# A convolution and attention network on one core: the order of the calls in a step of the attention stage, arranged anew

## The reference

```python
queries = conv1x1_bn(x, wq, sq, bq).reshape(b, NUM_HEADS, KEY_DIM, hw)   # 8 heads of 32
kv = conv1x1_bn(x, wkv, skv, bkv).reshape(b, KEY_DIM, hw)
key = jax.nn.softmax(kv, axis=2)
query = jax.nn.softmax(queries, axis=2)
context = jnp.einsum('bkn,bdn->bkd', key, kv)
attended = jnp.einsum('bkd,bhkn->bhdn', context, query).reshape(b, MQ, h, w)
x = x + conv1x1_bn(jax.nn.relu(attended), wp, sp, bp)
hdn = conv1x1_bn(x, w1, s1, b1)                        # 96 -> 384 channels
hdn = jax.nn.relu(depthwise_3x3(hdn, wdw) + bdw)
x = x + conv1x1_bn(hdn, w2, s2, b2)                    # 384 -> 96
```

## Time and profile before

| | |
|---|---|
| Time, median of 3 runs | 6700.78 us |
| The profiled execution: its own time | 6705.41 us |
| The profiled execution: span, mean granted TensorE clock | 6703.6 us, 0.981 |
| Busy share of the span: PE, DVE, POOL, ACT | 90%, 82%, 71%, 57% |
| Attention stage, from the start to the first instruction of the next stage | 0 to about 1828 us |

### The profile page before, as it was taken

The page is one execution under the profiler, slowest core; times in us unless marked ns, Lnnn a source line. Parts: engine busy times, 40 slices in busy tenths (PEclk is TensorE's granted clock), DMA queues, the critical chain, the costliest instruction groups (busy, mean ns, idle before and its releaser), DMA issues. The chain is left out here.

```text
span 6703.6 us, 228614 instructions
## 1 busy us (share of the span) xinstructions
PE 6053.1 (90%) x96819; PEld 3479.4 (52%) x96819; DVE 5507.3 (82%) x8016; ACT 3811.1 (57%) x5690; POOL 4761.0 (71%) x3268
## 2 busy tenths in 40 slices
PE   7999999999779999999999999999999999996877
PEld 3444444444345555555555555655555665553333
DVE  5776776776578888888888888888888888886998
ACT  3444444444346666656666655666665666664776
POOL 2344333334258888888888888888888888886766
PEclk9999999999889999999999999999999999998999
DMA  1111111111100000010000010000001000001221
GB/s 30 43 46 41 53 43 46 46 42 47 34 26 3 3 3 3 3 44 3 3 3 3 3 35 13 3 3 3 3 3 44 3 3 3 3 3 50 71 75 52
DMA packets 115654, 157.60 MB, mean 24 GB/s; under 512 B 30512, under 2 KB 79952, under 8 KB 114768
## 3 DMA queue, kind: packets, MB, share of 16 engines
q1 hardware_dynamic: 114768, 144.38, 7.6%
HBM read 53.67 MB, written 52.79 MB: 16 GB/s over the span
## 5 line engine op out<-in xcount | busy, mean ns | idle before, releaser
L241 ACT ACTIVATE nn_yy<-nn_P 128x612 f32<-128x612 f32 x1200 | 817.0, 681 | 1656.8 <-DVE nn_P L330 1639.3
L397 PE MATMUL nn_P<-nn_hh,nn_w 64*64 64x256 f16 x38400 | 1534.8, 273 | 220.6 <-DVE nn_nl L341 107.1
L209 POOL TENSOR_TENSOR nn_hf<-nn_hf,nn_sr 128x512 f32<-128x512 f32 (+1 forms) x800 | 1439.9, 1821 | 155.4 <-DVE nn_sr L363 155.4
L220 POOL TENSOR_TENSOR nn_hl<-nn_hf,nn_hh 128x512 f16<-128x512 f32 (+1 forms) x768 | 1266.2, 1649 | 314.5 <-ACT nn_hh L253 306.3
L397 PEld LDWEIGHTS nn_P<-nn_hh,nn_w 64*64 64x64 f16 x38400 | 1022.7, 106 | 834.0 <-issue 664.7
L404 PE MATMUL nn_P<-nn_nh,nn_w 64*64 64x512 f16 x19200 | 1320.6, 379 | 77.6 <-DVE nn_nl L341 8.8
L330 DVE SCALAR_TENSOR_TENSOR nn_P<-nn_P,nn_xs 128x612 f32<-128x612 f32 x1200 | 960.4, 800 | 234.2 <-PE nn_P L397 209.6
L336 DVE TENSOR_TENSOR nn_P<-nn_P,nn_nh 128x612 f32<-128x612 f32 x1200 | 960.2, 800 | 213.2 <-ACT nn_nh L246 206.8
L397 PE MATMUL nn_P<-nn_hl,nn_w 64*64 64x256 f16 x19200 | 994.0, 270 | 1.5 <-issue 1.2
L341 DVE SCALAR_TENSOR_TENSOR nn_nl<-nn_P,nn_nh 128x612 f16<-128x612 f32 x1200 | 952.1, 793 | 34.3
L246 ACT ACTIVATE nn_nh<-nn_yy 128x612 f16<-128x612 f32 x1200 | 856.1, 713 | 37.9
(11 more groups left out here) (215 smaller groups left out, 7986.1 us busy)
## 6 DMA issues: line engine op xcount, KB each, us to landing
xn_scratch<-at_xb SPq DMA_DIRECT2D x128, 114.8 KB
nn_xs<-xn_scratch SPq DMA_DIRECT2D x48, 306.0 KB, 3.0
at_x<-in_x SPq DMA_DIRECT2D x32, 384.0 KB, 3.8
x_scratch<-at_x SPq DMA_DIRECT2D x64, 192.0 KB, 2.1
h_scratch<-nn_hf SPq DMA_DIRECT2D x48, 256.0 KB, 3.1
ml_xt<-x_scratch SPq DMA_DIRECT2D x32, 384.0 KB, 4.4
ml_ht<-h_scratch SPq DMA_DIRECT2D x128, 96.0 KB
out<-ml_ot SPq DMA_DIRECT2D x64, 192.0 KB, 2.1
```

The source lines that it names most:

```text
L209: e.tensor_tensor(hf[c][:, g, :], hf[c][:, g, :], sr[c][:, :].unsqueeze(1).broadcast_to((128, g.stop - g.start, A_COLS)), ALU.mult).then_i ...
L220: e.tensor_tensor(hl[c][:, g, :], hf[c][:, g, :], hh[c][:, g, :], ALU.subtract).then_inc(h_lo[n], 1)
L241: e.activation(half(yy[k % RING][:, :]), Pv[k % 2], ACT.Ln).then_inc(logged, 1)
L397: return pe.matmul(out[:, 0:AC, rows_y] if near else out[:, 1:BC, rows_y], w1[rows, wp, a, 1 if near else 0, k, cols], (hh, hl)[dp][u][row ...
```

## The change

In `attention_block` the five `step` lists are rewritten but for SP's: POOL, ACT, DVE and PE call the same functions for the same images, in another order, and part of them one step later than before. No function, wait, tile or transfer is changed. What comes a step later: on PE the blocks from `conv(i1, 1, 2)` on, which become `conv(i2, 1, 2)` to `conv(i2, 5, 2)`, `mix` of the blocks 1 to 3 and `e_sum` of block 3 (now of `i1`), both `mlp_out`, and of the normalisation both `x_sum` and the second half's `centring` and `variance` (now of `i3`). PE's list before and after:

```diff
-                project(i1, 0); conv(i2, 4, 2); centring(i2, 0); conv(i2, 5, 0); project(i1, 1); variance(i2, 0); conv(i2, 5, 1)
-                keys(i0); conv(i2, 5, 2); q_rows(i0, 0); conv(i1, 0, 0); q_rows(i0, 1); conv(i1, 0, 1); mlp_out(i2, 1)
-                k_turn(i0); conv(i1, 0, 2); x_sum(i2, 0); q_cols(i0, 0); conv(i1, 1, 0); context(i0); q_cols(i0, 1)
...
+                mix(i1, 1); conv(i2, 1, 2); conv(i2, 2, 0); e_sum(i1, 3); conv(i2, 2, 1); mix(i1, 2); conv(i2, 2, 2); conv(i2, 3, 0)
+                mix(i1, 3); x_sum(i3, 0); project(i1, 0); keys(i0); centring(i3, 1); project(i1, 1); variance(i3, 1); conv(i2, 3, 1)
+                conv(i2, 3, 2); conv(i2, 4, 0); q_rows(i0, 0); conv(i2, 4, 1); mlp_out(i2, 0); q_rows(i0, 1); conv(i2, 4, 2); x_sum(i3, 1)
+                k_turn(i0); q_cols(i0, 0); conv(i2, 5, 0); q_cols(i0, 1); context(i0); centring(i2, 0); q_cols(i0, 2); conv(i2, 5, 1)
+                e_sum(i0, 0); variance(i2, 0); conv(i2, 5, 2); q_cols(i0, 3); e_sum(i0, 1); conv(i1, 0, 0); mix(i0, 0); conv(i1, 0, 1)
+                conv(i1, 0, 2); conv(i1, 1, 0); conv(i1, 1, 1); mlp_out(i2, 1); e_sum(i0, 2)
```

The other three lists of the change, of which the prediction speaks too (POOL, ACT, DVE):

```diff
+                a_low(i2, 1); a_low(i2, 2); a_low(i2, 3); x1_low(i2, 0); hidden_low(i3, 2); x1_low(i2, 1); e_low(i1, 0); hidden_low(i3, 3)
+                e_low(i1, 1); hidden_low(i3, 4); e_low(i1, 2); hidden_low(i3, 5); x_low(i0); e_low(i1, 3); hidden_low(i2, 0)
+                hidden_low(i2, 1); a_low(i1, 0)

+                x_high(i0); log_e(i1, 2); inv_e(i1, 2); a_high(i1, 0); relu(i2, 1); log_e(i1, 3); inv_e(i1, 3); a_high(i1, 1); relu(i2, 2)
+                log_x(i3, 0); a_high(i1, 2); a_high(i1, 3); inv_x(i3, 0); square(i3, 1); x1_high(i1, 0); log_var(i3, 1); inv_root(i3, 1)
+                k_exp(i0); spread(i0, 0); x1_high(i1, 1); spread(i0, 1); relu(i2, 3); log_x(i3, 1); q_exp(i0, 0); relu(i2, 4)
+                q_exp(i0, 1); e_high(i0, 0); square(i2, 0); e_high(i0, 1); log_e(i0, 0); inv_e(i0, 0); log_var(i2, 0); inv_root(i2, 0)
+                relu(i2, 5); log_e(i0, 1); inv_x(i3, 1); q_exp(i0, 2); q_exp(i0, 3); inv_e(i0, 1); e_high(i0, 2); e_high(i0, 3)
+                relu(i1, 0)

+                refine_e(i1, 2); attended(i1, 2); back_e(i1, 3); x2_make(i3, 1); floor(i3, 0); refine_e(i1, 3); attended(i1, 3)
+                hidden_high(i2, 2); sum_clamp(i3, 0); x1_make(i1, 0); k_max(i0); k_negate(i0); back_x(i3, 0); k_copy(i0); refine_x(i3, 0)
+                var_a(i3, 1); x1_make(i1, 1); var_b(i3, 1); refine_root(i3, 1); scale(i3, 1); q_max(i0, 0); k_inv(i0); affine(i3, 1)
+                floor(i3, 1); q_max(i0, 1); divide(i3, 0); sum_clamp(i3, 1); k_place(i0); hidden_high(i2, 3); x2_make(i2, 0)
+                hidden_high(i2, 4); context_scale(i0); block_diag(i0); back_e(i0, 0); refine_e(i0, 0); hidden_high(i2, 5); var_a(i2, 0)
+                var_b(i2, 0); back_e(i0, 1); refine_root(i2, 0); back_x(i3, 1); attended(i0, 0); hidden_high(i1, 0); scale(i2, 0)
+                refine_x(i3, 1); affine(i2, 0); refine_e(i0, 1); back_e(i0, 2); hidden_high(i1, 1); attended(i0, 1); divide(i3, 1)
```

More of the change, by code:

```diff
@@ L786, in step @@
             def step(n, p, t):
[L787 to L790, removed]
+                i0, i1, i2, i3, = image(n, p, t, 0), image(n, p, t, 1), image(n, p, t, 2), image(n, p, t, 3)
+                a_low(i2, 1); a_low(i2, 2); a_low(i2, 3); x1_low(i2, 0); hidden_low(i3, 2); x1_low(i2, 1); e_low(i1, 0); hidden_low(i3, 3)
+                e_low(i1, 1); hidden_low(i3, 4); e_low(i1, 2); hidden_low(i3, 5); x_low(i0); e_low(i1, 3); hidden_low(i2, 0)
+                hidden_low(i2, 1); a_low(i1, 0)
             images(e, step)
@@ L1243, in step @@
             def step(n, p, t):
-                i0, i1, i2 = (image(n, p, t, 0), image(n, p, t, 1), image(n, p, t, 2),)
-                project(i1, 0); conv(i2, 4, 2); centring(i2, 0); conv(i2, 5, 0); project(i1, 1); variance(i2, 0); conv(i2, 5, 1)
-                keys(i0); conv(i2, 5, 2); q_rows(i0, 0); conv(i1, 0, 0); q_rows(i0, 1); conv(i1, 0, 1); mlp_out(i2, 1)
-                k_turn(i0); conv(i1, 0, 2); x_sum(i2, 0); q_cols(i0, 0); conv(i1, 1, 0); context(i0); q_cols(i0, 1)
[L1248 to L1251, removed]
+                i0, i1, i2, i3, = image(n, p, t, 0), image(n, p, t, 1), image(n, p, t, 2), image(n, p, t, 3)
+                mix(i1, 1); conv(i2, 1, 2); conv(i2, 2, 0); e_sum(i1, 3); conv(i2, 2, 1); mix(i1, 2); conv(i2, 2, 2); conv(i2, 3, 0)
[4 more added lines that the diff above has]
+                conv(i1, 0, 2); conv(i1, 1, 0); conv(i1, 1, 1); mlp_out(i2, 1); e_sum(i0, 2)
             images(e, step)
```

## The result

The change takes 6770.22 us (median of 4 runs, 6757.91 to 6780.92), the kernel before 6701.39 beside it (4 runs, 6697.58 to 6705.15): 1.0102 times as long, 95% interval 1.0083 to 1.0121, or 69 us more. The forecast was 6750. The profiled execution of the change is its slowest, 6780.92 us; that of before took 6705.41.

The account below looks back on a forecast made before the run. PE was taken to bound the attention stage. Removed waits -81 us, `block_diag` +87, `x_sum` +39 and ends +6 gave +51, some 48 with roundings; from a median of 6700.8 this made 6750 us, range 6650 to 6772.

Parts of the forecast that it names:

- What bounds the kernel: Attention stage: PE bounds it; a step of 54.06 us would take 51.3 us without PE's three waits.
- What the order removes: PE's waits for `pack`'s DMAs, `a_low` and `sum_clamp` in each step all go: -2.8 us a step.
- Rival D: SP's queue: late x2 puts `pack` behind `conv(i1, 0, 0)`, each further us costing 29 us; above 6772 us, chance 0.08.
- `block_diag`, +2.9 a step: DVE's last four pieces wait out POOL's gapless run, so PE waits 2.9 us at `e_sum(i0, 0)`; ends 0 and 3.3.
- Rival A: At `block_diag` the subtractions get in and cost nothing, `x_sum` still waits: 6665 us (6650 to 6685), chance 0.24.
- `x_sum`, +1.3 a step: At the step's end POOL delays `divide` on DVE, so `x_sum(i3, 0)` starts 1.3 us late; ends 0 and 2.
- The ends: Pipeline's start and end: -6 and -3 at the start, +13 and +1.5 at the end, about +6 us.
- The sum: Whole kernel: -81, +87 for `block_diag`, +39 for `x_sum`, +6 at the ends, together +51 us, some 48 with roundings.

Follow-up runs that it names:

- experiment 7: The kernel of experiment 1 with POOL's `a_low(i1, 0)` moved ahead of `hidden_low(i2, 1)`: 6647.97 us, ratio to the kernel before 0.9918.
- experiment 8: The kernel of experiment 7 with `floor(i3, 0)` also ahead of `x2_make(i3, 1)` on DVE: 6647.93 us, ratio to the kernel before 0.9915.
- experiment 1: The change with `block_diag`'s eight pieces reading the context from PSUM, applying the reciprocal themselves: 6669.91 us, ratio to the kernel before 0.9951.
- experiment 12: The change itself run once more, nothing altered: 6764.18 us, last stage 583.9 us.

## Why the prediction was right, and where its parts were off

The forecast (slower, 6750) had the right sign and mechanism and was 20 us low. That it came so near is in part luck: the errors of its terms in the steady steps cancel, as the last point shows. The median of 6770.22 lies 2 us inside the upper end of the range given, 6772.

- **What bounds the kernel; 51.3 us a step without waits.** Right: 51.33 in experiments 7 and 8, with PE idle for 0.2 us in all.
- **What the order removes, -2.8 a step.** Right (54.06 - 51.33 = 2.73): none of the three waits is left in the steps, and `pack` is in time. Rival D (the DMAs) didn't come.
- **`block_diag`, +2.9 a step.** The place holds, and the size nearly: the wait is 2.33 us, and a step at clock 1.00 is 54.67, 2.55 above that of experiment 1. What the prediction gave as its value's reason failed: "If the subtractions don't get in, they end at 7.8", with the casts running by and the subtractions shut out. The casts are hit as well, and every piece gets in behind one POOL instruction; that was the other end of this term, 3.3. The two readings give nearly one sum, since in both the last pieces come behind POOL's fourth instruction. Rival A (the subtractions get in, 6665) was wrong in taking it that getting in after one instruction is cheap for eight pieces. Its 6665 is what the kernel does once the collision is taken away (experiment 1, 6670).
- **Why `back_x` misled.** Among the rows of single DVE instructions, those that waited out most of one POOL instruction and then let POOL do a further one first are `back_x` before the change (13 in all, where the prediction counted 14; two further ones), and after it `refine_x` (28, one further) and one `affine` (line 998, one further). All 42 had come in the middle of an `x_low` (97 x 1024). One of them, timeline after the change:

```profile
1167.59 2.12 POOL L758 TENSOR_TENSOR at_x<-at_x,at_x 97x1024 f16<-97x1024 f32 x1 [0.68 <-ACT at_x L803]
1167.71 3.66 DVE L1022 SCALAR_TENSOR_TENSOR at_nr<-at_nt,at_ny 96x512 f32<-96x512 f32 x1
1169.67 1.16 POOL L770 TENSOR_TENSOR at_e<-at_e,at_e 128x512 f16<-128x512 f32 x1
```

  `refine_x` arrives behind the start of `x_low`, `e_low` goes first too, and it ends at 1171.37. It is a scalar_tensor_tensor, so the operation isn't the distinction; and `back_x` itself, where it meets an `e_low` after the change, gets in behind it, 25 times of 25. Behind a POOL instruction of any other line DVE was let in after one, where it had come more than 0.2 us before its end. (The other `refine_x` of a step comes 0.05 to 0.17 us before the end of an `x1_low` and is done only behind the `hidden_low` that follows, 28 times; the rows don't tell whether it was passed over or asked too late.) Why `x_low` differs was not tried. In all 42 cases 1.3 us or more of it were left, and with the others at most 1.13, so it may be the length of what is waited out and not the line.
- **The clock.** Not foreseen: 15 of 29 steps at 0.97 or less, some 0.86 us a step in the mean (55.53 against 54.67), about 25 us. The prediction has no term for it: idleness at clock 1.00 is all that its rows showed, and it priced a longer wait by its length alone. This is the largest term that it lacks.
- **`x_sum`, +1.3 a step.** Right in place and cause (the `divide` that stands there takes 3.8 us, 1.32 alone; with it relieved in experiment 7 the wait is gone), too large: 0.6 of wait, 52.12 - 51.33 = 0.8 with the refilling.
- **The ends.** Start: -9 was forecast, -4.1 measured (-6.9 in experiment 8). End: +13, +1.5, and one `bd` and two `x_sum` waits, 20 in all, against +24.1. The counted work was right, 17 us forecast; PE's busy time there rises from 100.5 to 119.2. What failed is the credit "less the DMA wait and slow clock that the last image has now (-4)": the DMA wait falls from 3.8 to 1.0 us, but the granted clock of this way hardly rises (0.88 to 0.90), and PE's idle time in all rises from 28.6 to 34.0. Timeline of PE after the change, the last image, in answer to the earlier trace rows:

```profile
1853.00 0.38 PE L1136 MATMUL at_PC<-at_xr,at_w1T 105*128 105x512 f16 x1
1855.85 2.14 PE L1147 MATMUL at_PL<-at_hd,at_w2T 128*96 128x512 f16 x9 [2.47 <-POOL at_hd L764]
1861.55 2.02 PE L1164 MATMUL at_PL<-at_xm,at_sum_w 96*96 96x512 f32 x2 [3.56 <-DVE at_xm L1004]
...
1874.70 2.02 PE L1164 MATMUL at_PL<-at_xm,at_sum_w 96*96 96x512 f32 x2 [5.49 <-DVE at_xm L1004]
```

  The first half's `x_sum` now waits 3.56 us behind the last `mlp_out`, at the end of the pipeline where nothing stands in between; it is 3.57 in experiment 7 and 2.90 in 8, where `divide` is relieved, so most of it belongs to the order and not to `divide`.
- **The sum.** Steady +42.8 (forecast +40), start -4.1 (-9), end +24.1 (+20): 62.7 where the terms gave 51. The steady part, and with it the step of 55.53 us where 55.5 was said, is near by luck: over 29 steps `block_diag` is 10 us and `x_sum` 15 us too large, and the clock, worth 25, is missing. The two profiled executions differ by 75.5 us, and the 12.8 beside the 62.7 lie behind the attention stage, in code that isn't changed (the last stage alone took 582.7 and 595.7 us); experiment 12 shows the same program 12 us apart there. The medians differ by 69, and which part of that is the attention stage isn't known from the profiles.

On the ports: with their inputs in SBUF, the pieces that meet POOL need 1.1 us each, and with the context in PSUM all eight need 0.24. The Trainium skill, page "SBUF — State Buffer", section "Who interferes with whom", says that a DVE instruction with at most one SBUF input outside the two-port modes doesn't contend with GpSimd, that one with two SBUF inputs does where GpSimd reads SBUF, and that a cast can enter a two-port mode. The trace agrees with each: the pieces of experiment 1 aren't held up, the subtractions and casts of the change are (1.08 and 1.03 to 1.11 us). Experiment 1 changes the operation together with the operand's place. For the subtractions the place is what counts, since `refine_x` is a scalar_tensor_tensor too and waits with both tensors in SBUF; for the casts no run separates the two.

## What to carry to other kernels

A chain of small DVE instructions with SBUF inputs was here as dear as the POOL instructions it lay beside: count the pieces, and add one POOL instruction for each until POOL's run is over. Before an order puts such a chain late in front of a wait of the bounding engine, let it read its input from PSUM, or leave POOL a gap there; here the first turned a loss of 69 us into a gain of 30, the second into one of 9, and the first with POOL's `a_low` moved as well (experiment 7) into one of 59. A wait of the matrix engine can cost more than its length when the clock falls behind it, and the cost then differs from run to run.

## What the hardware showed that was not expected

- DVE instructions of 32 x 32 elements (0.17 to 0.18 us of their own) took 1.0 to 1.1 us each beside a gapless POOL run, one per POOL instruction.
- Leaving aside those that came less than 0.2 us before the end of a POOL instruction, a waiting DVE instruction was passed over by a further POOL instruction only where it had come in the middle of an `x_low` of 97 x 1024, 42 times of 42.
- With one idle time of 2.2 to 2.6 us in each step of 55 us the granted clock fell in 15 of 29 steps, and not in the others, in the same place of the same program; in the two repeats it was 13 and 18 (the second with 16 small matmuls more at the start). Filling it with ten useless matmuls made the kernel 32 us faster than the change.
- The last stage, which nothing changes, took 583.9 and 595.7 us in two executions of one program.
